# Sums of squares per row tile in column strips of TensorE, with partial adds of squares on GpSimd and VectorE, in the ternary feed-forward stages

## The chip, the core and the metric

The kernel runs on one core of a Trainium2 chip. The core has a matrix engine (PE, TensorE), three engines for elementwise work (DVE, VectorE; ACT, ScalarE; POOL, GpSimd) and a queue engine for transfers (SP, SyncE). The engines run their own instruction lists in order and meet at semaphores. The metric is the device time of one execution in microseconds.

## The reference

A residual stream `x` of 4096 rows (2 x 2048) by 256 passes through four stages: two layers of retention with a feed-forward part, a ternary feed-forward stage, windowed attention, and the ternary feed-forward stage again. The change is in the two ternary stages:

```
def _ternary_linear(x, w):
    alpha = jnp.mean(jnp.abs(w))
    w_t = jnp.sign(w) * (jnp.abs(w) > 0.5 * alpha).astype(w.dtype)
    w_q = w + jax.lax.stop_gradient(w_t - w)
    d = x.shape[-1]
    rms = jnp.sqrt(jnp.sum(x * x, axis=-1, keepdims=True)) / jnp.sqrt(jnp.asarray(d, x.dtype))
    x_norm = x / (rms + EPS)
    return jnp.einsum('bsd,fd->bsf', x_norm, w_q)
h = jax.nn.gelu(_ternary_linear(x, w_up), approximate=False)
return _ternary_linear(h, w_down)
```

The second product needs, for each of the 4096 rows, the mean of the squares of its 1024 hidden values. The kernel multiplies first and divides each output row by its rms afterwards.

## The kernel before

The function `ffn` is one stage. The names in the profile that begin with `ternary_ffn` belong to its two ternary calls. The 4096 rows are worked through in 8 blocks of 512 (`BT`); a block is 4 row tiles of 128. The hidden width of 1024 is 8 pieces of 128, counted by `m`. Hidden values stand transposed: 128 hidden channels on the partitions, 512 rows of the stream along the free axis.

Each engine has its own block of code with the same loop: `g` counts steps, `b = g - 2` is the block in work, `m` runs from 0 to 7. What an engine does, and in which order, is written out by hand with conditions on `m`; semaphores join the engines.

- PE, per `m`: `up_product(b, m)` (4 matmuls of 512 columns into `hp`, L679), then `down_product(b, m - 2)` (8 matmuls of 256 columns into `yp`, L690); for `m` of 0 and 1 it is the previous block's down products 6 and 7. Between them, at chosen `m`, stand the transposes of the next block's input (`tp`, L706), the sums of squares (`sqp`, L717) and the transposes of those sums (L724).
- ACT: `hidden` reads `hp` twice (L595 to `h`, L596 to `h_hi`); `odd_square` squares the pieces of odd `m` into `h_sq`; `sums_out` moves the sums to the SBUF tile `sq_sums`.
- DVE: `hidden_low` makes `h_lo = h - h_hi` (L433), which `down_product` needs; `residual` (L462) adds the finished block to the stream at the head of the block two later; `normalise` makes `xn` (L426); `statistics` and `aggregate` (L410, L418) go before the next block's scale; `mean_square` (L445).
- POOL: `even_square` squares the pieces of even `m` (L354); `squared_scales` and `last_scale` (L319 to L347) make the next block's scale; `rows_rms` (L359, L363) makes the rms that `residual` waits for.

The sums of squares. `h_sq` is 8 pieces of 128 x 512. `square_sums` has two halves of four pieces. In each, piece `s` of the half is the moving operand of one matmul with 32 columns of ones as weights, so that it uses one strip of 32 columns of the PE array and writes partitions `32 s` to `32 s + 31` of the bank `sqp`. After both halves strip `s` holds the sums over pieces `s` and `4 + s` for all 512 rows. ACT moves the bank, four transposes turn it, and a DVE reduction adds the four strips.

Of the kernel before, what the change touches and what calls it, by code (L numbers as in the profile page):

```python
# [25 lines left out]
P = 128  # L26
# [81 lines left out]
def ffn(nc, name, X, ident, lane, *, up, down, norm=None, hidden_bias=None, out_bias=None,  # L108
# [11 lines left out]
    with ExitStack() as c:  # L120
# [16 lines left out]
        if ternary:  # L137
            table_set = sb("table_set", [P, 1])
            h_sq = sb("h_sq", [P, MF, BT])
            sq_sums = sb("sq_sums", [P, BT])  # L140
# [47 lines left out]
        act_sq = sem("act_sq")  # L188
        sq_used = sem("sq_used")
# [80 lines left out]
        def _(pool):  # L270
# [85 lines left out]

            def rows_rms(b):
# [20 lines left out]
            def body(i):  # L378
                for k in range(2):
# [10 lines left out]
                    for m in range(0, MF, 2):  # L390
                        if live(b, NB):
                            even_square(b, m)
                        if m == 2 and unmeasured(g):
# [4 lines left out]
                        if m == 4 and live(b - 1, NB):  # L398
                            rows_rms(b - 1)
# [4 lines left out]
        def _(dve):  # L404
# [36 lines left out]

            def mean_square(b):
                dve.wait_ge(ms_full, b + 1)
                at_least(dve, rms_work, 2 * b - 1)
                nc.vector.tensor_reduce(ms[:, :], sqp[:, :].rearrange("p (t s e) -> p t s e", t=TB, e=SEG)[:, :, :, 0],  # L445
                                        axis=AX.X, op=ALU.add).then_inc(ms_done, 1)
# [98 lines left out]
            def body(i):  # L545
                for k in range(2):
                    g = 2 * i + k
                    b = g - 2
                    for m in range(MF):
# [32 lines left out]
        def _(act):  # L582
# [61 lines left out]
            def body(i):  # L644
                for k in range(2):
                    g = 2 * i + k
                    b = g - 2
                    for m in range(MF):
# [8 lines left out]
                        if m == 2 and ternary and live(b - 1, NB):  # L657
# [11 lines left out]
        def _(pe):  # L669
# [70 lines left out]
            def body(i):  # L740
                for k in range(2):
                    g = 2 * i + k
                    b = g - 2
                    for m in range(MF):
                        if live(b, NB):
                            up_product(b, m, k)
                        if ternary and m == (1 if last_block(b) else 2) and live(b - 1, NB):
# [5 lines left out]
                        if ternary and m == 4 and live(b - 1, NB):  # L753
# [1613 lines left out]
```

## Time and profile before

| | us |
|---|---|
| median of 3 runs | 1574.1 |
| the runs | 1572.0, 1574.1, 1576.66 |
| the profiled execution, its own time | 1573.14 |
| its span in the trace | 1571.4 |
| PE busy in the span | 1470.7 |
| DVE, ACT, POOL busy | 1020.5, 918.7, 765.0 |
| mean granted clock of TensorE | 0.973 of full |

The span is the time from the first to the last instruction of the profiled execution. Busy time of PE contains the pipeline latency of each matmul, so starts of successive rows tell more than durations. "Idle before" stands in brackets with what ended it. Columns of the timeline: start, duration, engine, line, operation, output and inputs, count. The ternary stages lie at about 913 to 1066 us and 1414 to 1571 us.

### The profile page before, as it was taken

What the parts mean: (1) busy time and instruction counts of PE and PEld (TensorE: products, weight loads), DVE (VectorE), ACT (ScalarE), POOL (GpSimd) and SP (SyncE); (2) the same over time, 40 slices, a digit from 0 to 9 for tenths busy, and PEclk for the clock granted to TensorE, in tenths of its full rate; (3) what the DMA queues carried; (4) which work ended last, traced back from release to release, by engine and by line L of the source; (5) the groups of instructions that cost most, each with busy time, mean ns of one, the idle gap of its engine ahead of it and who ended that gap; (6) DMA issues with size and microseconds to landing.
All of it is one profiled execution on the core that took longest, in us unless ns stands there. A gap on an engine that the chain in (4) does not pass through costs nothing. (4 is left out here: it accounts for less than half of the span.)

```text
span 1571.4 us, 36208 instructions
## 1 busy us (share of the span) xinstructions
PE 1470.7 (94%) x12834; PEld 1202.5 (77%) x12834; DVE 1020.5 (65%) x2266; ACT 918.7 (58%) x1728; POOL 765.0 (49%) x826
## 2 busy tenths in 40 slices
PE   4999997999998999997999989995999999989998
PEld 3777875889886788876989878884777777768786
DVE  4877775554436877874655757663777777756664
ACT  4565553555544555445555556663777777756665
POOL 2566765111104666664313335543666666635553
PEclk9999998899999999998999999997999999999999
DMA  7000000100001000002000010000000000000101
GB/s 238 2 2 1 0 1 1 34 1 1 1 1 55 2 2 0 2 1 94 28 28 14 1 38 1 0 1 1 1 1 0 0 0 0 1 1 1 41 27 42
DMA packets 21089, 26.17 MB, mean 17 GB/s; under 512 B 1904, under 2 KB 19056, under 8 KB 20848
## 3 DMA queue, kind: packets, MB, share of 16 engines
q1 hardware_dynamic: 18432, 21.64, 4.1%
q10 hardware_dynamic: 2544, 3.04, 0.6%
q8 instruction: 69, 1.13, 0.3%
q14 instruction: 44, 0.36, 0.1%
HBM read 20.48 MB, written 4.19 MB: 16 GB/s over the span
## 5 line engine op out<-in xcount | busy, mean ns | idle before, releaser
L595 ACT ACTIVATE ffn_h<-ffn_hp,c_b 128x512 f32<-128x512 f32 x128 | 88.3, 690 | 171.5 <-PE ffn_hp L679 171.2
L433 DVE TENSOR_TENSOR ffn_h_lo<-ffn_h,ffn_h_hi 128x512 fp32r<-128x512 f32 x128 | 93.7, 732 | 144.1 <-ACT ffn_h_hi L596 144.0
L433 DVE TENSOR_TENSOR ternary_ffn_h_lo<-ternary_ffn_h,ternary_ffn_h_hi 128x512 fp32r<-128x512 f32 x128 | 97.7, 763 | 110.4 <-ACT ternary_ffn_h_hi L596 109.6
L690 PE MATMUL ffn_yp<-down_hi,ffn_h_hi 128*128 128x256 f32 x512 | 145.5, 284 | 0.0
L690 PE MATMUL ffn_yp<-down_hi,ffn_h_lo 128*128 128x256 f32 x512 | 142.8, 279 | 0.0
L690 PE MATMUL ffn_yp<-down_lo,ffn_h_hi 128*128 128x256 f32 x512 | 142.8, 279 | 0.0
L690 PE MATMUL ternary_ffn_yp<-down_ternary,ternary_ffn_h_hi 128*128 128x256 f32 x512 | 132.7, 294 | 0.0
L986 POOL TENSOR_TENSOR ret_qk<-ret_qk,ret_qk_sin 128x512 f32<-128x512 f32 x64 | 82.7, 1292 | 102.6 <-DVE ret_qk_sin L1083 101.9
L595 ACT ACTIVATE ternary_ffn_h<-ternary_ffn_hp 128x512 f32<-128x512 f32 x128 | 76.6, 598 | 95.8 <-PE ternary_ffn_hp L679 91.7
L354 POOL TENSOR_TENSOR ternary_ffn_h_sq<-ternary_ffn_h 128x512 f32<-128x512 f32 x64 | 79.4, 1241 | 105.3 <-ACT ternary_ffn_h_hi L596 105.3
L690 PE MATMUL ternary_ffn_yp<-down_ternary,ternary_ffn_h_lo 128*128 128x256 f32 x512 | 125.5, 280 | 0.0
L992 POOL TENSOR_TENSOR ret_rstd<-ret_sums,ret_minus_half 128x16 f32<-128x16 f32 x32 | 103.7, 3241 | 44.0 <-DVE ret_sums L1125 44.0
L1710 POOL TENSOR_TENSOR wa_rms<-wa_rms,win_minus_half 128x20 f32<-128x20 f32 x32 | 119.1, 3722 | 2.7
L690 PEld LDWEIGHTS ternary_ffn_yp<-down_ternary,ternary_ffn_h_hi 128*128 128x128 f32 x512 | 96.9, 189 | 29.2 <-issue 26.0
L1930 ACT ACTIVATE wa_probs_t<-wa_tp 128x512 f32<-128x512 f32 x128 | 76.4, 597 | 62.7 <-PE wa_tp L2100 62.2
L679 PE MATMUL ternary_ffn_hp<-xt_hi,up_ternary 128*128 128x512 f32 x256 | 103.7, 405 | 4.3 <-DVEq L578 4.3
L679 PE MATMUL ffn_hp<-xt_hi,up_hi 128*128 128x512 f32 x256 | 102.6, 401 | 4.4 <-DVEq L578 4.4
L679 PE MATMUL ternary_ffn_hp<-xt_lo,up_ternary 128*128 128x512 f32 x256 | 103.9, 406 | 0.0
L679 PE MATMUL ffn_hp<-xt_lo,up_hi 128*128 128x512 f32 x256 | 102.4, 400 | 0.0
L308 POOL TENSOR_SCALAR ffn_scale_work<-mean_var 128x4 f32<-128x4 f32 x13 | 3.6, 280 | 202.5 <-DVE mean_var L418 202.5
L679 PE MATMUL ffn_hp<-xt_hi,up_lo 128*128 128x512 f32 x256 | 102.0, 398 | 0.0
L690 PEld LDWEIGHTS ffn_yp<-down_lo,ffn_h_hi 128*128 128x128 f32 x512 | 96.4, 188 | 4.3
(265 smaller groups left out, 4619.6 us busy)
## 6 DMA issues: line engine op xcount, KB each, us to landing
X<-in_x SPq DMA_DIRECT2D x8, 512.0 KB, 10.1
staging<-in_w SPq DMA_DIRECT2D x4, 1024.0 KB, 9.1
ffn_x_in<-in_x SPq DMA_DIRECT2D x8, 512.0 KB, 3.8
out<-X SPq DMA_DIRECT2D x7, 512.0 KB, 2.9
rotary<-in_rotary ACTq DMA_DIRECT2D x1, 1024.0 KB, 7.2
staging<-in_w_up SPq DMA_DIRECT2D x1, 1024.0 KB, 4.8
staging<-in_w_down SPq DMA_DIRECT2D x1, 1024.0 KB, 8.2
staging<-in_wqkv ACTq DMA_DIRECT2D x1, 768.0 KB, 6.0
```

The costliest lines, as they stand in the source:

```text
L308: nc.gpsimd.tensor_scalar(work[:, 0, :], mv[:, k, :, 1], EPS, None, ALU.add).then_inc(work_done, 1)
L354: nc.gpsimd.tensor_tensor(h_sq[:, m, :], h[:, m % R, :], h[:, m % R, :], ALU.mult).then_inc(pool_sq, 1)
L433: nc.vector.tensor_tensor(h_lo[:, m % R, :], h[:, m % R, :], h_hi[:, m % R, :].bitcast(F32), ALU.subtract).then_inc(h_ready, 1)
L595: nc.scalar.activation(h[:, m % R, :], hp[m % 2][:, :], fn, bias=bias)
L679: last = nc.tensor.matmul(hp[m % 2][:, :], w[:, j, m * P:(m + 1) * P], x[:, k, j, :], start=(n == 0), stop=(n == len(todo) - 1))
L690: last = nc.tensor.matmul(yp[k][t // 2][:, (t % 2) * D:(t % 2 + 1) * D], x[:, m % R, t * P:(t + 1) * P], w[:, m, :], start=(m == 0 and t % ...
L986: nc.gpsimd.tensor_tensor(qk[:, r, :, :, :], qk[:, r, :, :, :], qk_sin[:, r, :, :, :], ALU.add).then_inc(qk_done, 1)
L992: nc.gpsimd.tensor_tensor(rstd[:, :], sums[:, 1, :], minus_half[:, :], ALU.pow).then_inc(rstd_done, 1)
L1710: nc.gpsimd.tensor_tensor(rms[:, 1, :], rms[:, 0, :], minus_half[:, :], ALU.pow).then_inc(rms_work, 1)
L1930: nc.scalar.activation(pt[:, g, :, :].rearrange("p c n -> p (c n)"), tp[:, :], ACT.Copy).then_inc(pt_done, 1)
```

## The change

- Squares are added before PE sums them. POOL adds piece 1 onto 0 (`add_01`, behind the square of piece 2) and then 2 onto 0 (`add_0123`, behind the square of piece 4) and 5 onto 4 (`add_45`). DVE adds 3 onto 2 (`add_23`, at `m` of 4), and, in the next block at `m` of 1, 7 onto 6 and 6 onto 4 (`add_67`, `add_4567`). In the last block of a stage the second half is not added: PE reads its four pieces.
- `square_sums` takes one added piece per half. Row tile `t` of it (128 columns) goes to strip `t`, in place of piece `s` (512 columns) to strip `s`. The sums stand in the first 128 columns of `sqp`.
- One transpose turns them, in place of four; ACT moves 128 x 128; DVE copies four columns (`tensor_copy`) in place of the reduction.
- Places: PE's second half moves from `m` of 2 to 3, the transpose from 4 to 5, the first half from 6 to 7; `sums_out` from 2 to 4, `mean_square` from 4 to 5, `rows_rms` from 4 to 6.

```
+            def add_01(b):
+                pool.wait_ge(pool_sq, MF // 2 * b + 1)
+                pool.wait_ge(act_sq, MF // 2 * b + 1)
+                nc.gpsimd.tensor_tensor(h_sq[:, 0, :], h_sq[:, 0, :], h_sq[:, 1, :], ALU.add).then_inc(sq_01, 1)
+
+            def add_0123(b):
+                pool.wait_ge(sq_01, b + 1)
+                pool.wait_ge(sq_23, b + 1)
+                nc.gpsimd.tensor_tensor(h_sq[:, 0, :], h_sq[:, 0, :], h_sq[:, 2, :], ALU.add).then_inc(sq_0123, 1)
+
+            def add_45(b):
+                pool.wait_ge(pool_sq, MF // 2 * b + 3)
+                pool.wait_ge(act_sq, MF // 2 * b + 3)
+                nc.gpsimd.tensor_tensor(h_sq[:, 4, :], h_sq[:, 4, :], h_sq[:, 5, :], ALU.add).then_inc(sq_45, 1)
...
                         if live(b, NB):
                             even_square(b, m)
+                            if m == 2:
+                                add_01(b)
+                            if m == 4:
+                                add_0123(b)
+                                if not final_block(b):
+                                    add_45(b)
...
-                        if m == 4 and live(b - 1, NB):
+                        if m == 6 and live(b - 1, NB):
                             rows_rms(b - 1)
...
+            def add_23(b):
+                dve.wait_ge(pool_sq, MF // 2 * b + 2)
+                dve.wait_ge(act_sq, MF // 2 * b + 2)
+                nc.vector.tensor_tensor(h_sq[:, 2, :], h_sq[:, 2, :], h_sq[:, 3, :], ALU.add).then_inc(sq_23, 1)
+
+            def add_67(b):
+                dve.wait_ge(pool_sq, MF // 2 * (b + 1))
+                dve.wait_ge(act_sq, MF // 2 * (b + 1))
+                nc.vector.tensor_tensor(h_sq[:, 6, :], h_sq[:, 6, :], h_sq[:, 7, :], ALU.add).then_inc(sq_67, 1)
+
+            def add_4567(b):
+                dve.wait_ge(sq_45, b + 1)
+                dve.wait_ge(sq_67, b + 1)
+                nc.vector.tensor_tensor(h_sq[:, 4, :], h_sq[:, 4, :], h_sq[:, 6, :], ALU.add).then_inc(sq_4567, 1)
...
-                nc.vector.tensor_reduce(ms[:, :], sqp[:, :].rearrange("p (t s e) -> p t s e", t=TB, e=SEG)[:, :, :, 0],
-                                        axis=AX.X, op=ALU.add).then_inc(ms_done, 1)
+                nc.vector.tensor_copy(ms[:, :], sqp[:, 0:P].rearrange("p (t e) -> p t e", e=SEG)[:, :, 0]
+                                      ).then_inc(ms_done, 1)
...
-                        if m == 4 and ternary and live(b - 1, NB):
+                        if m == 5 and ternary and live(b - 1, NB):
                             mean_square(b - 1)
+                        if m == 4 and ternary and live(b, NB):
+                            add_23(b)
+                        if m == 1 and ternary and live(b - 1, NB) and not final_block(b - 1):
+                            add_67(b - 1)
+                            add_4567(b - 1)
...
             def square_sums(b, half):
 
-                done = MF // 2 * b + 2 * (half + 1)
-                pe.wait_ge(act_sq, done)
-                pe.wait_ge(pool_sq, done)
+                if half == 1 and final_block(b):
+                    pe.wait_ge(act_sq, MF // 2 * (b + 1))
+                    pe.wait_ge(pool_sq, MF // 2 * (b + 1))
+                    whole_rows = (4, 5, 6, 7)
+                else:
+                    pe.wait_ge(sq_4567 if half else sq_0123, b + 1)
+                    whole_rows = (4 * half,)
                 if half == 0:
                     at_least(pe, ms_done, b)
-                for s in range(4):
-                    last = nc.tensor.matmul(sqp[SEG * s:SEG * (s + 1), :], ones[:, :], h_sq[:, 4 * half + s, :],
-                                            start=(half == 0), stop=(half == 1))
+                for m in whole_rows:
+                    for t in range(TB):
+                        last = nc.tensor.matmul(sqp[SEG * t:SEG * (t + 1), 0:P], ones[:, :], h_sq[:, m, t * P:(t + 1) * P],
+                                                start=(half == 0), stop=(half == 1 and m == whole_rows[-1]))
                 last.then_inc(sums_full if half else sq_used, 1)
...
-                        if ternary and m == (1 if last_block(b) else 2) and live(b - 1, NB):
+                        if ternary and m == (1 if last_block(b) else 3) and live(b - 1, NB):
                             square_sums(b - 1, 1)
```

DVE at the head of a block of the first ternary stage, from the reciprocal for `residual` to the second pair of `statistics`, before:

```order
L451 RECIPROCAL ternary_ffn_inv_rms<-ternary_ffn_rms 128x4
L462 SCALAR_TENSOR_TENSOR X<-ternary_ffn_yp,ternary_ffn_inv_rms,X 128x256 x4
L433 TENSOR_TENSOR ternary_ffn_h_lo<-ternary_ffn_h,ternary_ffn_h_hi 128x512
L426 TENSOR_SCALAR xn<-X,mean_var,scale 128x256 x4
L433 TENSOR_TENSOR ternary_ffn_h_lo<-ternary_ffn_h,ternary_ffn_h_hi 128x512
L410 BN_STATS ternary_ffn_stats<-X 128x6 x2
L433 TENSOR_TENSOR ternary_ffn_h_lo<-ternary_ffn_h,ternary_ffn_h_hi 128x512
L410 BN_STATS ternary_ffn_stats<-X 128x6 x2
L418 BN_AGGR mean_var<-ternary_ffn_stats 128x2 x4
```

and now:

```order
L494 RECIPROCAL ternary_ffn_inv_rms<-ternary_ffn_rms 128x4
L505 SCALAR_TENSOR_TENSOR X<-ternary_ffn_yp,ternary_ffn_inv_rms,X 128x256 x4
L461 TENSOR_TENSOR ternary_ffn_h_lo<-ternary_ffn_h,ternary_ffn_h_hi 128x512
L454 TENSOR_SCALAR xn<-X,mean_var,scale 128x256 x4
L461 TENSOR_TENSOR ternary_ffn_h_lo<-ternary_ffn_h,ternary_ffn_h_hi 128x512
L438 BN_STATS ternary_ffn_stats<-X 128x6 x2
L478 TENSOR_TENSOR ternary_ffn_h_sq<-ternary_ffn_h_sq 128x512
L483 TENSOR_TENSOR ternary_ffn_h_sq<-ternary_ffn_h_sq 128x512
L461 TENSOR_TENSOR ternary_ffn_h_lo<-ternary_ffn_h,ternary_ffn_h_hi 128x512
L438 BN_STATS ternary_ffn_stats<-X 128x6 x2
L446 BN_AGGR mean_var<-ternary_ffn_stats 128x2 x4
L461 TENSOR_TENSOR ternary_ffn_h_lo<-ternary_ffn_h,ternary_ffn_h_hi 128x512
```

The adds L478 (`add_67`) and L483 (`add_4567`) now stand between the first pair of `statistics` and `h_lo` of piece 2.

POOL from the squares of pieces 0 and 2 on (`x2`), before; the row ahead of them is `last_scale`:

```order
L347 TENSOR_TENSOR scale<-ternary_ffn_scale_work,ternary_ffn_powers 128x4
L354 TENSOR_TENSOR ternary_ffn_h_sq<-ternary_ffn_h 128x512 x2
L319 TENSOR_SCALAR ternary_ffn_scale_work<-mean_var 128x4
L320 TENSOR_TENSOR ternary_ffn_scale_work<-mean_var,ternary_ffn_powers 128x4
L322 TENSOR_TENSOR ternary_ffn_scale_work<-ternary_ffn_scale_work,ternary_ffn_powers 128x4
L326 TENSOR_SCALAR ternary_ffn_scale_work<-ternary_ffn_scale_work 128x4
L329 TENSOR_TENSOR ternary_ffn_scale_work<-ternary_ffn_scale_work 128x4
L354 TENSOR_TENSOR ternary_ffn_h_sq<-ternary_ffn_h 128x512
L359 TENSOR_TENSOR ternary_ffn_rms<-ternary_ffn_mean_square,ternary_ffn_powers 128x4
L363 TENSOR_SCALAR ternary_ffn_rms<-ternary_ffn_rms 128x4
```

and now, without the row of `last_scale`:

```order
L361 TENSOR_TENSOR ternary_ffn_h_sq<-ternary_ffn_h 128x512 x2
L367 TENSOR_TENSOR ternary_ffn_h_sq<-ternary_ffn_h_sq 128x512
L326 TENSOR_SCALAR ternary_ffn_scale_work<-mean_var 128x4
L327 TENSOR_TENSOR ternary_ffn_scale_work<-mean_var,ternary_ffn_powers 128x4
L329 TENSOR_TENSOR ternary_ffn_scale_work<-ternary_ffn_scale_work,ternary_ffn_powers 128x4
L333 TENSOR_SCALAR ternary_ffn_scale_work<-ternary_ffn_scale_work 128x4
L336 TENSOR_TENSOR ternary_ffn_scale_work<-ternary_ffn_scale_work 128x4
L361 TENSOR_TENSOR ternary_ffn_h_sq<-ternary_ffn_h 128x512
L372 TENSOR_TENSOR ternary_ffn_h_sq<-ternary_ffn_h_sq 128x512
L377 TENSOR_TENSOR ternary_ffn_h_sq<-ternary_ffn_h_sq 128x512
L361 TENSOR_TENSOR ternary_ffn_h_sq<-ternary_ffn_h 128x512
L381 TENSOR_TENSOR ternary_ffn_rms<-ternary_ffn_mean_square,ternary_ffn_powers 128x4
```

Three adds over the tile of squares are new (L367, L372, L377), and the rms L381 stands behind the square of piece 6, not of piece 4.

PE around the second half of the sums, before (behind up product 2):

```order
L679 MATMUL ternary_ffn_hp<-xt_hi,up_ternary 128x512
L679 MATMUL ternary_ffn_hp<-xt_lo,up_ternary 128x512
L712 ISA
L717 MATMUL ternary_ffn_sqp<-ternary_ffn_h_sq,ternary_ffn_ones 32x512 x4
L690 MATMUL ternary_ffn_yp<-down_ternary,ternary_ffn_h_hi 128x256
L690 MATMUL ternary_ffn_yp<-down_ternary,ternary_ffn_h_lo 128x256
```

and now (behind up product 3; `tp` are the transposes of the next block's input):

```order
L727 MATMUL ternary_ffn_hp<-xt_hi,up_ternary 128x512
L727 MATMUL ternary_ffn_hp<-xt_lo,up_ternary 128x512
L770 MATMUL ternary_ffn_sqp<-ternary_ffn_h_sq,ternary_ffn_ones 32x128 x4
L754 MATMUL ternary_ffn_tp<-c_ident,xn 128x128 x4
L738 MATMUL ternary_ffn_yp<-down_ternary,ternary_ffn_h_hi 128x256
L738 MATMUL ternary_ffn_yp<-down_ternary,ternary_ffn_h_lo 128x256
```

The group now stands one up product and one down product later, ahead of the input's transposes, and its matmuls have 128 columns.

## Rows read from the trace of the kernel before

**Rows 1.** The page: busy time and granted clock in 40 slices

```profile
PE 1470.7 (94%) x12834; PEld 1202.5 (77%) x12834; DVE 1020.5 (65%) x2266; ACT 918.7 (58%) x1728; POOL 765.0 (49%) x826
...
PEclk9999998899999999998999999997999999999999
```

**Rows 2.** The table by stretches: one block of the first ternary stage

```profile
core 0: us, PE busy (x) PEld busy (x) DVE busy (x) ACT busy (x) POOL busy (x), PEclk, DMA share, GB/s
990.67:1009.30 18.63, 18.63 (x127) 14.81 (x125) 12.18 (x28) 12.48 (x24) 9.91 (x13) 1.00 0.00 0
```

**Rows 3.** Timeline of PE (start, duration; idle before in brackets)

```profile
990.67 0.40 PE L679 MATMUL ternary_ffn_hp<-xt_hi,up_ternary 128*128 128x512 f32 x1
...
992.52 0.40 PE L679 MATMUL ternary_ffn_hp<-xt_hi,up_ternary 128*128 128x512 f32 x1
...
995.08 0.40 PE L679 MATMUL ternary_ffn_hp<-xt_lo,up_ternary 128*128 128x512 f32 x1
995.41 1.06 PE L717 MATMUL ternary_ffn_sqp<-ternary_ffn_h_sq,ternary_ffn_ones 128*32 128x512 f32 x8
996.41 0.39 PE L690 MATMUL ternary_ffn_yp<-down_ternary,ternary_ffn_h_hi 128*128 128x256 f32 x1
996.63 0.28 PE L690 MATMUL ternary_ffn_yp<-down_ternary,ternary_ffn_h_lo 128*128 128x256 f32 x1
996.75 0.28 PE L690 MATMUL ternary_ffn_yp<-down_ternary,ternary_ffn_h_hi 128*128 128x256 f32 x1
```

**Rows 4.** Timeline of PE, a cut of 0.1 us at the start of one group

```profile
986.77 0.64 PE L717 MATMUL ternary_ffn_sqp<-ternary_ffn_h_sq,ternary_ffn_ones 128*32 128x512 f32 x4
```

**Rows 5.** Timeline of PE, the four transposes of the sums

```profile
1000.69 0.60 PE L724 MATMUL ternary_ffn_sqp<-c_ident,ternary_ffn_sq_sums 128*128 128x128 f32 x4
1001.04 0.36 PE L690 MATMUL ternary_ffn_yp<-down_ternary,ternary_ffn_h_hi 128*128 128x256 f32 x1
```

**Rows 6.** Timeline of DVE over the head of that block

```profile
992.17 1.66 DVE L462 SCALAR_TENSOR_TENSOR X<-ternary_ffn_yp,ternary_ffn_inv_rms,X 128x256 f32 x4 [0.25 <-DVE ternary_ffn_inv_rms L451]
993.75 1.05 DVE L433 TENSOR_TENSOR ternary_ffn_h_lo<-ternary_ffn_h,ternary_ffn_h_hi 128x512 fp32r<-128x512 f32 x1
994.73 1.37 DVE L426 TENSOR_SCALAR xn<-X,mean_var,scale 128x256 f32 x4
...
996.63 0.73 DVE L410 BATCH_NORM_STATS2 ternary_ffn_stats<-X 128x6 f32 x2
997.29 1.19 DVE L433 TENSOR_TENSOR ternary_ffn_h_lo<-ternary_ffn_h,ternary_ffn_h_hi 128x512 fp32r<-128x512 f32 x1
```

**Rows 7.** Timeline of POOL over the same block

```profile
993.22 1.04 POOL L354 TENSOR_TENSOR ternary_ffn_h_sq<-ternary_ffn_h 128x512 f32<-128x512 f32 x1 [2.48 <-ACT ternary_ffn_h_hi L596]
996.89 1.04 POOL L354 TENSOR_TENSOR ternary_ffn_h_sq<-ternary_ffn_h 128x512 f32<-128x512 f32 x1 [2.63 <-ACT ternary_ffn_h_hi L596]
999.95 0.61 POOL L319 TENSOR_SCALAR ternary_ffn_scale_work<-mean_var 128x4 f32<-128x4 f32 x1 [2.02 <-DVE mean_var L418]
...
1004.32 1.04 POOL L359 TENSOR_TENSOR ternary_ffn_rms<-ternary_ffn_mean_square,ternary_ffn_powers 128x4 f32<-128x4 f32 x1
```

**Rows 8.** Timelines of DVE and of POOL where both start together

```profile
988.15 0.69 DVE L433 TENSOR_TENSOR ternary_ffn_h_lo<-ternary_ffn_h,ternary_ffn_h_hi 128x512 fp32r<-128x512 f32 x1 [1.08 <-ACT ternary_ffn_h_hi L596]
...
988.20 1.54 POOL L354 TENSOR_TENSOR ternary_ffn_h_sq<-ternary_ffn_h 128x512 f32<-128x512 f32 x1 [1.09 <-ACT ternary_ffn_h_hi L596]
```

**Rows 9.** Groups by form on POOL: busy, mean ns of one, idle before

```profile
L986 POOL TENSOR_TENSOR ret_qk<-ret_qk,ret_qk_sin 128x512 f32<-128x512 f32 x64 | 82.7, 1292 | 102.6 <-DVE ret_qk_sin L1083 101.9
L354 POOL TENSOR_TENSOR ternary_ffn_h_sq<-ternary_ffn_h 128x512 f32<-128x512 f32 x64 | 79.4, 1241 | 105.3 <-ACT ternary_ffn_h_hi L596 105.3
```

**Rows 10.** Stretches at 910 us, and PE's timeline there

```profile
910.00:913.40 3.40, 1.28 (x9) 1.04 (x9) 1.32 (x2) 0.77 (x1) 0.79 (x6) 0.99 0.00 0
913.40:916.80 3.40, 3.40 (x10) 2.61 (x9) 0.69 (x1) 2.19 (x5) 2.58 (x5) 0.50 0.88 266
...
912.93 0.50 PE L679 MATMUL ternary_ffn_hp<-xt_hi,up_ternary 128*128 128x512 f32 x1 [2.12 <-DVEq L578]
```

More of the change, by code:

```diff
@@ L95, in last_block, with final_block @@
     return isinstance(b, int) and b == NB
+def final_block(b):
+    return isinstance(b, int) and b == NB - 1
 def after_last(b):
@@ L139, in ffn @@
             h_sq = sb("h_sq", [P, MF, BT])
-            sq_sums = sb("sq_sums", [P, BT])
+            sq_sums = sb("sq_sums", [P, P])
             ones = sb("ones", [P, SEG])
@@ L188, in ffn @@
         act_sq = sem("act_sq")
+        sq_01, sq_23, sq_0123 = sem("sq_01"), sem("sq_23"), sem("sq_0123")
+        sq_45, sq_67, sq_4567 = sem("sq_45"), sem("sq_67"), sem("sq_4567")
         sq_used = sem("sq_used")
@@ L623, in sums_out @@
                 at_least(act, ms_full, b)
-                nc.scalar.activation(sq_sums[:, :], sqp[:, :], ACT.Copy, scale=1.0 / FF).then_inc(sums_moved, 1)
+                nc.scalar.activation(sq_sums[:, :], sqp[:, 0:P], ACT.Copy, scale=1.0 / FF).then_inc(sums_moved, 1)
             def for_next_stage(g, m):
@@ L656, in body @@
                             odd_square(b, m)
-                        if m == 2 and ternary and live(b - 1, NB):
+                        if m == 4 and ternary and live(b - 1, NB):
                             sums_out(b - 1)
@@ L722, in transpose_sums @@
                 pe.wait_ge(sums_moved, b + 1)
-                for t in range(TB):
-                    last = nc.tensor.transpose(sqp[:, t * P:(t + 1) * P], sq_sums[:, t * P:(t + 1) * P], ident[:, :])
-                last.then_inc(ms_full, 1)
+                nc.tensor.transpose(sqp[:, 0:P], sq_sums[:, :], ident[:, :]).then_inc(ms_full, 1)
             def weight_total():
@@ L752, in body @@
                             transposes(g - 1, 1)
-                        if ternary and m == 4 and live(b - 1, NB):
+                        if ternary and m == 5 and live(b - 1, NB):
                             transpose_sums(b - 1)
-                        if ternary and m == 6 and live(b, NB):
+                        if ternary and m == 7 and live(b, NB):
                             square_sums(b, 0)
```

## The prediction

> **What bounds the kernel now.** I read the page first: PE is busy 1470.7 of 1571.4 us and is granted close to full clock nearly everywhere [rows 1]. The table by stretches then shows one block of a ternary stage, from the start of one up product 0 to the next: 18.63 us, PE busy in all of them at a clock of 1.00, DVE 12.2, ACT 12.5, POOL 9.9 [rows 2]. So PE's own work sets a block, and an instruction taken from PE is time won for as long as nothing else makes PE wait. An up product and the down product behind it take 992.52 - 990.67 = 1.85 us, 0.93 and 0.92 [rows 3]. Eight pairs make 14.8 us; the other 3.8 are the two groups of sums, two groups of input transposes and the group of four transposes of the sums.
>
> **What PE saves.** A group of sums: the last matmul of the up product starts at 995.08 and the group at 995.41; 0.23 would be the usual step (0.93 / 4), so 0.10 is lost there. The next down matmul starts at 996.41 and its second 0.22 later where 0.12 is usual [rows 3]. The group costs 0.10 + 1.00 + 0.10 = 1.20 us. Four matmuls start within 0.64 - 0.60 = 0.04 us of each other [rows 4] (0.60 is one such matmul's duration), so the strips run side by side, and the eight records are two passes. Of the 1.00, two passes of 512 columns would take 2 x 0.43 = 0.86 if a column is worth what one lasts at 1.00 less the tail of 0.14. With 128 columns a pass is a quarter: 0.21. A group then costs 1.20 - 0.64 = 0.56. The bounds: the saving is at most 0.86 (the columns free), and it is at least 0.30 if eight short matmuls can start no faster than those four transposes do, 0.35 / 4 = 0.09 each [rows 5], 0.70 in all in place of 1.00. I take 0.64, since four starts within 0.04 us are the nearest row. Three of four transposes go: 3 x 0.09 = 0.26 [rows 5]. A block so loses 2 x 0.64 + 0.26 = 1.54 us of PE work: 17.1 in place of 18.63. Over 16 blocks that would be 24 us, were nothing late.
>
> The Trainium skill, page "TensorE: Matmul & The Clock Gate", section "Wait — 56ns, not 53.3ns?", says that with hardware decoding off the sequencer spends about 62 ns on each matmul and that this binds once the array's work is shorter. By it eight records would take 0.50 and the saving would be 0.36 a group, some 9 us less over both stages; the row with four starts in 0.04 us speaks against it, though those may have been decoded ahead.
>
> **What is late: the second half of the sums.** Count from the start of up product 0 (t = 0, 990.67 in the rows). PE now asks for `sq_4567` after four up and three down products, t = 4 x 0.93 + 3 x 0.92 = 6.5. DVE has to do `add_67` and `add_4567` before that, behind the first pair of `statistics`. In the rows that pair is done, and the next instruction starts, at 997.29, t = 6.6 [rows 6]. So even with nothing in the way the two adds end at t = 8.0: each is 0.69 as `h_lo` alone [rows 8], the first 0.61 up to the next start (`xn` starts 0.07 ahead of the end of `h_lo` [rows 6]), and I allow 0.1 for the hand-overs by semaphore. So PE waits 1.5 us. That alone eats the 1.54.
>
> And something is in the way. DVE's `h_lo` and POOL's square, both with 128x512 operands in SBUF, don't run at once: POOL's square lasts 1.04 alone [rows 7], and 1.54 where DVE began 0.05 before it [rows 8]; DVE's `h_lo` lasts 0.69 alone [rows 8], and 1.05 and 1.19 where POOL's squares of 993.22 and 996.89 were under way [rows 6, 7]: each ends about 0.6 behind the end of the square. The adds on either engine are of this form. POOL's square of piece 2 holds from t = 6.2 to 7.2 [rows 7], and `add_01` is queued right behind it with all its inputs ready. So from t = 7.2 `add_67`, `add_01` and `add_4567` go one after another, in whichever order. For `add_01` I have two rows: 1.04 for a square, whose two inputs are one tile, and 1.29 for `ret_qk`, a sum of two tiles of this size [rows 9]; it is the second that an add resembles: 1.29. The sum: 7.2 + 0.61 + 1.29 + 0.69 + 0.1 = 9.9. PE waits 3.4 us, between 1.5 (nothing shared) and 4.1 (all of DVE 0.7 later, as `residual` is below).
>
> The Trainium skill, page "SBUF — State Buffer", section "Who interferes with whom", states this as an exclusive lock on a port pair for a DVE instruction with two SBUF inputs against a GpSimd one that reads SBUF. The rows above agree. By a kernel in which they shared bandwidth, the wait would be nearer to 1.5.
>
> **What is queued behind.** `h_lo` of piece 2 waits on DVE behind the adds, to about t = 10.6 in place of 7.8, the statistics and the aggregate behind it too, and with them POOL's scale, which began at 999.95, t = 9.3 [rows 7], and now begins near 12. POOL then has squares 4 and 6, two adds of 1.29 and the rms, about 6 us, back to back, with 3.4 us of scale ahead: the rms moves from 13.7 (1004.32) [rows 7] to the first microseconds of the next block. `residual`, which starts at t = 1.5 now (992.17) [rows 6], starts near 2.2, and `h_lo` of piece 0 behind it is some 0.3 us late for its down product. ACT's narrower move, DVE's copy and the later places of both are hidden under PE's products: they cost nothing as long as the rms is there by the head of the next block, else the sum above.
>
> **The sum.** A full block: 18.63 - 1.54 + 3.4 + 0.3 = 20.8, 2.15 more than before. Each stage has six such blocks (the second halves of blocks 1 to 6): 12 x 2.15 = 26. Block 0's half comes where DVE has no `residual` yet, so its wait is nearer 1.5: nothing gained or lost. The final block asks for no adds in its second half and saves one group and the transposes, 0.9, twice: -2. Together +24 us.
>
> **The clock.** After PE had stood for 2.12 us before 912.93, the granted clock was 0.50, that is 1.2 GHz, for the next 3.4 us [rows 10]. A wait of 3.4 each block shows as an idle of some 3.2, longer than that one. If each of the 12 costs a stretch of 3.4 us at half clock, up to 1.7 us of work is lost each time, less what of the stretch lies in the wait itself. I take 0.9: +11 us. The bounds are 0 and 20.
>
> Profiled execution 1573.1 + 24 + 11 = 1608; the median stands 1 us above it, so 1609.
>
> **Rivals.**
> (a) As forecast, 1600 to 1620: chance 0.45.
> (b) The same waits, but shorter or without the fall of the clock: `add_01` at 1.04 and a wait of 3.1 gives 1573 + 12 x 1.8 - 2 = 1593; waits as forecast and full clock give 1598. 1579 to 1600: chance 0.33.
> (c) Faster. DVE reaches the adds earlier, or the adds of the two engines don't hold each other up. If PE's wait is 0.8 where I have 3.4, a block is 17.9, and 14 blocks x -0.7 - 2 = -13: 1561. It turns at a wait of 1.5 us. What speaks for it: PE's new order gives all engines other phases, and in the rows DVE has idle time of its own (12.2 busy of 18.63). Against it: that idle time is not at the head of a block, where `residual`, `xn` and `statistics` fill it from 992.17 to 997.29 [rows 6]. 1550 to 1569: chance 0.17.
> (d) The wait is about 1.5 and nothing changes, 1570 to 1579: 0.05.
>
> About 0.3%, 5 us, is what a measurement of this kernel can tell from no change. Slower by more than that: 0.45 + 0.33 = 0.78; within it 0.05; faster 0.17. The range of 1573 to 1620 leaves out (c) and the ends of (a) and (d), about 0.2.
>
> **What the profile after would show.** Right: a group of sums at 0.2 to 0.35 us between its start and the next; PE's stop before `sqp` in the second half, released by a DVE add over `h_sq`, some 3 us, 12 times, and about 1.5 twice; blocks of 20.5 to 22.5 us; DVE's adds stretched beyond 0.69 beside POOL's of about 1.3; stretches of clock 0.50 behind the stops. Wrong if: blocks are 17 to 18 us; POOL's adds last 1.04; the clock stays at 1.00 through the stops; or PE stops elsewhere, at `h_lo` for instance.

## The result, and the profile after

The changed kernel takes 1605.1 us (median of 4 runs, 1600.3 to 1606.5), the kernel before 1573.05 beside it: a ratio of 1.0198, 95% interval 1.0165 to 1.0231. It is slower by 32 us, and the interval lies clear of 1; forecast was 1609, with 0.78 on slower. Its profiled execution took 1603.9, the span is 1602.0 us.

The page, the lines of [rows 1]:

```profile
PE 1458.0 (91%) x12802; PEld 1208.4 (75%) x12834; DVE 1085.5 (68%) x2310; ACT 914.9 (57%) x1728; POOL 838.7 (52%) x872
...
PEclk9999997999999999979999989997999999999998
```

PE is busy 12.7 us less and yet the span is 30.6 longer; DVE gained 65 us of work, POOL 74. The table by stretches, from one second group of sums to the next, which is one block as in [rows 2] (twice in the first ternary stage, once in the second):

```profile
core 0: us, PE busy (x) PEld busy (x) DVE busy (x) ACT busy (x) POOL busy (x), PEclk, DMA share, GB/s
966.89:988.91 22.02, 18.86 (x121) 15.87 (x121) 16.09 (x32) 12.15 (x23) 15.67 (x15) 0.92 0.01 1
988.91:1010.63 21.72, 17.27 (x121) 14.38 (x121) 16.91 (x32) 12.26 (x23) 14.61 (x15) 1.00 0.00 1
1477.61:1498.22 20.61, 17.26 (x121) 14.37 (x121) 16.08 (x32) 12.26 (x23) 15.72 (x15) 1.00 0.08 27
```

A block took 18.63; now 20.6 to 22.0, of which PE works 17.3 at full clock. Where it stands, from PE's timeline (start, duration, idle before in brackets), beside [rows 3] and [rows 4]:

```profile
966.89 0.43 PE L770 MATMUL ternary_ffn_sqp<-ternary_ffn_h_sq,ternary_ffn_ones 128*32 128x128 f32 x8 [2.86 <-DVE ternary_ffn_h_sq L483]
...
978.79 0.39 PE L727 MATMUL ternary_ffn_hp<-xt_hi,up_ternary 128*128 128x512 f32 x1
...
983.99 0.39 PE L738 MATMUL ternary_ffn_yp<-down_ternary,ternary_ffn_h_hi 128*128 128x256 f32 x1 [0.38 <-DVE ternary_ffn_h_lo L461]
...
988.91 0.42 PE L770 MATMUL ternary_ffn_sqp<-ternary_ffn_h_sq,ternary_ffn_ones 128*32 128x128 f32 x8 [2.78 <-DVE ternary_ffn_h_sq L483]
989.27 0.44 PE L754 MATMUL ternary_ffn_tp<-c_ident,xn 128*128 128x128 f32 x2
...
1005.04 0.38 PE L738 MATMUL ternary_ffn_yp<-down_ternary,ternary_ffn_h_hi 128*128 128x256 f32 x1 [0.99 <-DVE ternary_ffn_h_lo L461]
...
1010.63 0.42 PE L770 MATMUL ternary_ffn_sqp<-ternary_ffn_h_sq,ternary_ffn_ones 128*32 128x128 f32 x8 [3.46 <-DVE ternary_ffn_h_sq L483]
```

The group itself is short (0.36 to the next start, 1.00 before). Ahead of it PE stands until `add_4567` (L483) is done, and at the head of the block it also stands at down product 0, for `h_lo`. The view of the tile `h_sq` counts the first kind and gives each add's least, median and longest duration:

```profile
L367 POOL TENSOR_TENSOR ternary_ffn_h_sq<-ternary_ffn_h_sq x16: 1307/1707/1741, 922.0 to 1582.7; 128x512 f32<-128x512 f32 x16
...
L377 POOL TENSOR_TENSOR ternary_ffn_h_sq<-ternary_ffn_h_sq x14: 1284/1293/1741, 932.9 to 1572.7; 128x512 f32<-128x512 f32 x14
L478 DVE TENSOR_TENSOR ternary_ffn_h_sq<-ternary_ffn_h_sq x14: 667/864/1444, 941.4 to 1580.4; 128x512 f32<-128x512 f32 x14
L483 DVE TENSOR_TENSOR ternary_ffn_h_sq<-ternary_ffn_h_sq x14: 691/1566/1568, 942.7 to 1581.2; 128x512 f32<-128x512 f32 x14
...
  PE ternary_ffn_sqp L770: 37.1, 13
```

DVE's timeline at the end of the stretch before 988.91, beside [rows 6]:

```profile
981.60 1.66 DVE L505 SCALAR_TENSOR_TENSOR X<-ternary_ffn_yp,ternary_ffn_inv_rms,X 128x256 f32 x4 [0.25 <-DVE ternary_ffn_inv_rms L494]
...
985.66 0.74 DVE L438 BATCH_NORM_STATS2 ternary_ffn_stats<-X 128x6 f32 x2
986.33 0.87 DVE L478 TENSOR_TENSOR ternary_ffn_h_sq<-ternary_ffn_h_sq 128x512 f32<-128x512 f32 x1
987.30 1.56 DVE L483 TENSOR_TENSOR ternary_ffn_h_sq<-ternary_ffn_h_sq 128x512 f32<-128x512 f32 x1
```

and POOL's, beside [rows 7]:

```profile
980.90 0.23 POOL L385 TENSOR_SCALAR ternary_ffn_rms<-ternary_ffn_rms 128x4 f32<-128x4 f32 x1 [0.22 <-POOL ternary_ffn_rms L381]
...
985.03 1.61 POOL L361 TENSOR_TENSOR ternary_ffn_h_sq<-ternary_ffn_h 128x512 f32<-128x512 f32 x1 [1.88 <-ACT ternary_ffn_h_hi L644]
986.61 1.70 POOL L367 TENSOR_TENSOR ternary_ffn_h_sq<-ternary_ffn_h_sq 128x512 f32<-128x512 f32 x1
```

`add_67` ends at 987.20, 0.56 behind the end of POOL's square (986.64); `add_4567` ends at 988.86, 0.55 behind the end of `add_01` (988.31), and PE starts 0.05 later. Of PE's three microseconds DVE needs 1.4 for the adds alone (two of 0.69); the rest is DVE and POOL taking turns. DVE's `statistics`, just ahead of them, kept their 0.74 although POOL's square ran beside them.

### The profile page after: what moved, and what is told of

Same layout as the page of the kernel before. It is cut to its first block and busy times, and to the rows that moved or that the text cites. A ratio compares the mean times of both kernels' runs of the same rounds, so it can differ in the third digit from the quotient of the medians.

```text
span 1602.0 us, 36348 instructions
## 1 busy us (share of the span) xinstructions
PE 1458.0 (91%) x12802; PEld 1208.4 (75%) x12834; DVE 1085.5 (68%) x2310; ACT 914.9 (57%) x1728; POOL 838.7 (52%) x872
## 5 line engine op out<-in xcount | busy, mean ns | idle before, releaser
L461 DVE TENSOR_TENSOR ternary_ffn_h_lo<-ternary_ffn_h,ternary_ffn_h_hi 128x512 fp32r<-128x512 f32 x128 | 110.8, 869 | 61.5 <-ACT ternary_ffn_h_hi L644 61.5
L738 PE MATMUL ternary_ffn_yp<-down_ternary,ternary_ffn_h_hi 128*128 128x256 f32 x512 | 136.9, 300 | 4.0 <-DVE ternary_ffn_h_lo L461 4.0
L738 PE MATMUL ternary_ffn_yp<-down_ternary,ternary_ffn_h_lo 128*128 128x256 f32 x512 | 130.2, 288 | 0.0
L738 PEld LDWEIGHTS ternary_ffn_yp<-down_ternary,ternary_ffn_h_hi 128*128 128x128 f32 x512 | 101.8, 199 | 15.3 <-DVE X L505 5.2
L361 POOL TENSOR_TENSOR ternary_ffn_h_sq<-ternary_ffn_h 128x512 f32<-128x512 f32 x64 | 84.3, 1317 | 49.0 <-ACT ternary_ffn_h_hi L644 48.9
L738 PEld LDWEIGHTS ternary_ffn_yp<-down_ternary,ternary_ffn_h_lo 128*128 128x128 f32 x512 | 101.7, 199 | 3.2
## 6 DMA issues: line engine op xcount, KB each, us to landing
X<-in_x SPq DMA_DIRECT2D x8, 512.0 KB, 10.1
```

The costliest lines, as they stand in the source:

```text
L361: nc.gpsimd.tensor_tensor(h_sq[:, m, :], h[:, m % R, :], h[:, m % R, :], ALU.mult).then_inc(pool_sq, 1)
L461: nc.vector.tensor_tensor(h_lo[:, m % R, :], h[:, m % R, :], h_hi[:, m % R, :].bitcast(F32), ALU.subtract).then_inc(h_ready, 1)
L738: last = nc.tensor.matmul(yp[k][t // 2][:, (t % 2) * D:(t % 2 + 1) * D], x[:, m % R, t * P:(t + 1) * P], w[:, m, :], start=(m == 0 and t % ...
```

## The experiments

In all of them the places of the groups, the transpose, `sums_out`, `mean_square` and `rows_rms` are those of the change unless the diff says otherwise; times are medians; each ratio is against the kernel before, timed beside that run, with its 95% interval.

**No adds.** PE reads all four pieces of each half, in column strips, with one transpose.

```
-                            if m == 2:
-                                add_01(b)
...
-                if half == 1 and final_block(b):
-                    pe.wait_ge(act_sq, MF // 2 * (b + 1))
-                    pe.wait_ge(pool_sq, MF // 2 * (b + 1))
-                    whole_rows = (4, 5, 6, 7)
+                if True:
+                    pe.wait_ge(act_sq, MF // 2 * b + 2 * (half + 1))
+                    pe.wait_ge(pool_sq, MF // 2 * b + 2 * (half + 1))
+                    whole_rows = tuple(range(4 * half, 4 * half + 4))
```

> Row tiles in strips, one transpose, and every place moved as in the change, but no adds: PE reads four pieces in each half (16 matmuls of 128 columns). Theory A (the adds make PE wait): PE's groups cost as before, 1.2 us, three transposes a block go, 16 x 0.26 = 4 us, so 1569 and no wait of PE on the sums. Rival C (the later places of the rms, the move and the transpose delay `residual` and with it everything): waits of PE on `h_lo` or on xn stay and the time is 1580 or more. Rival B (more and narrower matmuls are dearer than counted, sequencer-bound): the group takes 2 us or more in place of 1.0, the time 1590 or more.

1565.34 against 1572.19: 0.9961 (0.9949 to 0.9974). A block in the table by stretches:

```profile
988.20:1006.41 18.21, 18.21 (x177) 15.73 (x173) 12.80 (x28) 12.26 (x24) 10.30 (x13) 1.00 0.00 0
```

The second half's group in PE's timeline:

```profile
996.61 1.08 PE L759 MATMUL ternary_ffn_sqp<-ternary_ffn_h_sq,ternary_ffn_ones 128*32 128x128 f32 x32
997.62 0.55 PE L743 MATMUL ternary_ffn_tp<-c_ident,xn 128*128 128x128 f32 x3
```

A group lasts 1.01, as before: 32 records in place of 8, with a quarter of the columns each. The block loses 0.42, where the three transposes explain 0.26; the other 0.16 comes with the places. The late places of the sums and of the rms alone cost nothing: PE shows no wait for the sums or for `h_lo` in this run's ternary stages.

**Adds in the first half only** (`add_01`, `add_23`, `add_0123`; the second half whole).

```
-                                if not final_block(b):
-                                    add_45(b)
...
-                            add_67(b - 1)
-                            add_4567(b - 1)
...
+                if half == 1:
```

> The change, with the adds of the first half alone (two on POOL, one on DVE); the second half is read whole by PE, 16 matmuls of 128 columns. Theory A: nothing is added at the head of a block, where DVE is full, so PE waits for no add; a block loses 0.64 + 0.26 = 0.9 us, 16 blocks 14 us: 1559, at full clock through the ternary stages. Rival A' (it is the port pair taken by any add, wherever it stands, that costs): DVE's h_lo and POOL's squares of pieces 4 to 6 get late, and the time stays at 1575 or above. Rival C: as in the run without adds, 1580 or more.

1562.82, 0.9942 (0.9925 to 0.9959). Blocks are a steady 17.57, so narrowing a group is worth 18.21 - 17.57 = 0.64. One block, the second of the first ternary stage, took 22.9: PE stood for `add_0123` there. In PE's timeline:

```profile
956.15 0.43 PE L765 MATMUL ternary_ffn_sqp<-ternary_ffn_h_sq,ternary_ffn_ones 128*32 128x128 f32 x8 [3.08 <-POOL ternary_ffn_h_sq L372]
```

and in POOL's, 7 us earlier:

```profile
949.04 3.14 POOL L329 TENSOR_TENSOR ternary_ffn_scale_work<-ternary_ffn_scale_work,ternary_ffn_powers 128x4 f32<-128x4 f32 x1
```

L329 normally lasts 1.01. In that block DVE also mixes the next stage's weights (L552), so that from 948.39 to 951.65 it ran instructions with two inputs without a pause.

**Adds in the second half only** (`add_45`, `add_67`, `add_4567`; the first half whole).

```
+                if half == 0 or final_block(b):
```

> The change, with the adds of the second half alone (one on POOL behind the square of piece 4, two on DVE at m of 1); the first half is read whole. Theory A: the wait before the second half's sums stays, about 2 to 2.5 us (no add_01 between the two DVE adds any more, and POOL is free earlier), 12 times, with some falls of the clock: 1573 - 14 + 12 x 2.2 + 5 = 1590. Rival A' (the number of adds counts, not where): half of the change's loss, less than 1582.

1589.54, 1.0117 (1.01 to 1.0134). This half alone loses 17 us, about half of the change's 32, where the first half alone gained 9. PE waits 2.0 in most blocks (13 waits, 1.1 to 2.0, together 23.8), although `add_01` is gone. With the first half's adds put back the 13 waits are 37.1: adds that gain when they stand alone cost 16 us (1589.5 to 1605.1) beside the second half's. So the second half alone makes half of the loss, and the other half arises only where both are present. Two neighbouring blocks in the table by stretches, alike but for the clock:

```profile
963.91:983.54 19.63, 17.62 (x145) 15.06 (x145) 14.10 (x31) 12.14 (x23) 11.57 (x13) 1.00 0.01 3
983.54:1004.71 21.17, 19.18 (x145) 16.59 (x146) 13.96 (x31) 12.25 (x23) 12.11 (x13) 0.92 0.00 0
```

A fall of the clock behind the wait costs 21.17 - 19.63 = 1.54 us.

**The six adds over 4 of their 512 columns**: the instructions, waits and places stay, the work goes. What is summed is no longer the squares of all pieces: only 4 of 512 rows get all of them, in this run and the next two each for the adds that are cut.

```
-                nc.gpsimd.tensor_tensor(h_sq[:, 0, :], h_sq[:, 0, :], h_sq[:, 1, :], ALU.add).then_inc(sq_01, 1)
+                nc.gpsimd.tensor_tensor(h_sq[:, 0, 0:4], h_sq[:, 0, 0:4], h_sq[:, 1, 0:4], ALU.add).then_inc(sq_01, 1)
```

> The change with its order, semaphores and narrow groups, but each of the six adds works on 4 of 512 columns, so the sums leave out most of the squares' adds. Theory A: the adds' work is what PE waits for; with 0.1 us each PE waits 0.2 us a block at most, and the narrow groups show their worth: 1573 - 24 + 4 = 1553. Rival D (the new waits and hand-overs by semaphore cost, not the work): 1575 or more. Rival B: the narrow group saves less than 0.64, then 1560 or more with no wait of PE.

1557.21, 0.9903 (0.9887 to 0.992). PE still waits; a block in the table by stretches:

```profile
980.41:998.34 17.93, 16.99 (x122) 14.45 (x122) 12.23 (x32) 12.17 (x24) 10.66 (x15) 1.00 0.00 1
```

Its end in PE's timeline:

```profile
998.34 0.43 PE L770 MATMUL ternary_ffn_sqp<-ternary_ffn_h_sq,ternary_ffn_ones 128*32 128x128 f32 x8 [0.94 <-DVE ternary_ffn_h_sq L483]
```

and in DVE's:

```profile
997.55 0.47 DVE L478 TENSOR_TENSOR ternary_ffn_h_sq<-ternary_ffn_h_sq 128x4 f32<-128x4 f32 x1
998.12 0.16 DVE L483 TENSOR_TENSOR ternary_ffn_h_sq<-ternary_ffn_h_sq 128x4 f32<-128x4 f32 x1
```

and in POOL's:

```profile
996.96 1.04 POOL L361 TENSOR_TENSOR ternary_ffn_h_sq<-ternary_ffn_h 128x512 f32<-128x512 f32 x1 [2.44 <-ACT ternary_ffn_h_hi L644]
```

PE falls idle at 998.34 - 0.94 = 997.40 and DVE reaches the adds 0.15 later. The first one lasts 0.47, though such a short add lasts 0.15 where nothing holds it: it ends just behind POOL's square (998.00). That hold, the late start and the hand-overs are the 0.9 above the 16.99 of work. There are 12 such waits, together 10.3 us where I had allowed 4, which more than covers the 4 us that I missed (the saving was larger too). The full adds cost 1605.1 - 1557.2 = 48 us; waits and hand-overs by semaphore alone don't make the loss.

**Only POOL's adds over 4 columns, and only DVE's.** The same edit, to three adds each.

> The change with POOL's three adds over 4 of 512 columns (so the sums leave those adds out) and DVE's three adds whole. With all six short the block was 17.9 us, with PE waiting about 1.1 for DVE's adds. Theory A (both DVE's own queue and POOL's add between): DVE's two adds bring 2 x 0.6 more, so PE waits about 2.3 and a block is 19.1; some waits are followed by a fall of the clock: 1578, between 1572 and 1585. Rival (POOL's adds are nothing, it is DVE's alone): as the change, 1600 or more. Rival (only the clash matters): as all short, 1557 to 1562.

> The change with DVE's three adds over 4 of 512 columns and POOL's three whole. Theory A: DVE's short adds still queue behind POOL's square of piece 2 and add_01 (up to 1.04 + 1.29) and `xn` and the rms stay late, so PE waits 1.5 to 2.5 a block: 1575, between 1566 and 1585. Rival (it is DVE's time that counts): 1557 to 1562. Rival (it is POOL's time alone): 1595 or more.

1584.66, 1.0081 (1.0064 to 1.0098), and 1582.38, 1.0068 (1.0051 to 1.0085). DVE's adds alone cost 27 us over those with all six cut, POOL's alone 25; together 48. Neither queue is the whole cause. With DVE's adds alone, in PE's timeline:

```profile
982.16 0.43 PE L770 MATMUL ternary_ffn_sqp<-ternary_ffn_h_sq,ternary_ffn_ones 128*32 128x128 f32 x8 [2.01 <-DVE ternary_ffn_h_sq L483]
```

and in DVE's:

```profile
980.08 1.23 DVE L478 TENSOR_TENSOR ternary_ffn_h_sq<-ternary_ffn_h_sq 128x512 f32<-128x512 f32 x1
981.41 0.69 DVE L483 TENSOR_TENSOR ternary_ffn_h_sq<-ternary_ffn_h_sq 128x512 f32<-128x512 f32 x1
```

With POOL's adds alone, in PE's timeline:

```profile
1004.10 0.48 PE L770 MATMUL ternary_ffn_sqp<-ternary_ffn_h_sq,ternary_ffn_ones 128*32 128x128 f32 x8 [2.49 <-DVE ternary_ffn_h_sq L483]
```

in DVE's:

```profile
999.28 2.10 DVE L454 TENSOR_SCALAR xn<-X,mean_var,scale 128x256 f32 x4
1001.30 1.76 DVE L461 TENSOR_TENSOR ternary_ffn_h_lo<-ternary_ffn_h,ternary_ffn_h_hi 128x512 fp32r<-128x512 f32 x1
```

and in POOL's:

```profile
1000.19 1.04 POOL L361 TENSOR_TENSOR ternary_ffn_h_sq<-ternary_ffn_h 128x512 f32<-128x512 f32 x1 [1.38 <-ACT ternary_ffn_h_hi L644]
1001.19 1.32 POOL L367 TENSOR_TENSOR ternary_ffn_h_sq<-ternary_ffn_h_sq 128x512 f32<-128x512 f32 x1
```

`h_lo` takes 1.76 and ends 0.55 behind POOL's `add_01`, and what queues behind it is late. The medians lie 6.7 and 7.4 above what I expected. The waits were about as long as I had taken them (2.0 in most blocks with DVE's adds, 1.7 to 1.9 and once 2.5 with POOL's); in the profiled executions 6 and 8 of them were followed by a stretch at the clock's lower level, which I had priced low. How much of the 7 us is the clock's isn't separated, and the profiled execution with DVE's adds alone, 1579.65, is itself 5 below its median.

**DVE's second-half adds ahead of the first pair of `statistics`.** This asks whether what stands ahead of the adds in DVE's queue (Theory A) makes the wait.

```
+                        if m == 1 and ternary and live(b - 1, NB) and not final_block(b - 1):
+                            add_67(b - 1)
+                            add_4567(b - 1)
                         if 1 <= m < 3 and unmeasured(g):
                             statistics(g, 2 * m - 2)
```

> The change with add_67 and add_4567 ahead of the first pair of statistics on DVE instead of behind. Theory A (PE waits for what stands ahead of the adds on DVE): the two statistics of 0.67 us together come off the wait, 12 times, and a fall of the clock or two may go: 1605 - 8 - 3 = 1594. Rival (the moment is set by POOL's square of piece 2 and add_01 on the port pair): nothing gained, 1602 to 1608.

1602.87, 1.0195 (1.0178 to 1.0212): 2 us less than the change where Theory A gave 11. DVE's timeline in one block:

```profile
1005.36 2.17 DVE L454 TENSOR_SCALAR xn<-X,mean_var,scale 128x256 f32 x4
1007.45 1.75 DVE L461 TENSOR_TENSOR ternary_ffn_h_lo<-ternary_ffn_h,ternary_ffn_h_hi 128x512 fp32r<-128x512 f32 x1
1009.13 0.68 DVE L478 TENSOR_TENSOR ternary_ffn_h_sq<-ternary_ffn_h_sq 128x512 f32<-128x512 f32 x1
```

The 0.7 us of `statistics` are no longer ahead, but `h_lo` now meets POOL's square and `add_01` (`h_lo` 1.75 for 0.69), so the adds begin no sooner. That holds for this block and four like it, where PE waited 2.8 to 3.0 as before. In the others the new place did help; two waits in PE's timeline:

```profile
956.13 0.44 PE L770 MATMUL ternary_ffn_sqp<-ternary_ffn_h_sq,ternary_ffn_ones 128*32 128x128 f32 x4 [3.08 <-POOL ternary_ffn_h_sq L372]
...
1032.47 0.32 PE L770 MATMUL ternary_ffn_sqp<-ternary_ffn_h_sq,ternary_ffn_ones 128*32 128x128 f32 x4 [1.73 <-DVE ternary_ffn_h_sq L483]
```

The waits for `add_4567` fell from 37.1 to 25.5 us in all (12 of them, seven between 1.0 and 1.9). About half of that came back elsewhere: 3.1 for `add_0123` in block 1 (the wait before 956.13), 1.8 more for `h_lo` and 0.9 more for the first `xn`; where the rest went isn't traced. So the place in DVE's queue sets part of the wait, which the median alone would hide.

**The first half added, but for block 1**, where the weights are mixed: `first half only` with that block whole.

```
+                            if m == 2 and not second_block(b):
+                                add_01(b)
...
+                if half == 1 or second_block(b):
```

> The version with the first half's adds alone, in which PE waited 3.1 us once: block 1 of the first ternary stage, where DVE also mixes the attention weights and POOL's power took 3.1 us. Here block 1 of each stage is read whole in both halves. If that one wait and the clock's fall behind it are what held that version back: 1562.8 - 3.1 - 1.5 + 2 x 0.64 = 1559.5. If not: 1562 or above.

1557.68 (1556.27 to 1558.0), 0.9901 (0.9885 to 0.9918): faster than both kernels, by 15 us and 47. Against the run without adds (1565.34) the first half's adds are worth 8 or 9 of the 15; the rest is the one transpose and the places. In the table by stretches a block has PE at work throughout:

```profile
978.80:996.37 17.57, 17.57 (x153) 15.09 (x149) 13.07 (x30) 12.17 (x24) 13.43 (x15) 1.00 0.00 0
```

**That, with `add_45` on POOL too**; PE reads three pieces in the second half. (In block 1's second half piece 5 is left out of the sum.)

```
+                    if half == 1 and not final_block(b) and not second_block(b):
+                        pe.wait_ge(sq_45, b + 1)
+                        whole_rows = (4, 6, 7)
```

> The version with the first half's adds (block 1 whole), and POOL's add_45 besides, so that PE reads three pieces (4 with 5 added, 6, 7) in the second half of all blocks but 1 and the last. Each saves PE 0.21 us, 12 times 2.6 us, so 1555 if nothing is late. Rival: POOL has 1.3 to 1.7 us more ahead of the square of piece 6, the rms and the scale; the rms, for which DVE already waits 0.6 at the head of a block, moves 1.3 later, `residual` and the first h_lo with it, and PE waits for h_lo: 1558 or above. I hold this rival likelier, since POOL's add stands where the rms is next.

1573.1 against 1573.25, 0.9998 (0.9989 to 1.0006). One more add on POOL (1.27 at the least, 1.74 in the median of its 12) eats the whole gain of 15 us, without any of DVE's second-half adds. Nothing waits for `add_45` itself: down product 0 stands for `h_lo` (9 waits, 9.6 us in all), and the first half's group of the same block for `add_0123` (L377, 2.9 us in all), which comes later on POOL than before. In PE's timeline:

```profile
996.75 0.38 PE L746 MATMUL ternary_ffn_yp<-down_ternary,ternary_ffn_h_hi 128*128 128x256 f32 x1 [1.26 <-DVE ternary_ffn_h_lo L470]
...
1009.01 0.43 PE L781 MATMUL ternary_ffn_sqp<-ternary_ffn_h_sq,ternary_ffn_ones 128*32 128x128 f32 x8 [0.40 <-POOL ternary_ffn_h_sq L377]
```

**The change with the rms ahead of `add_45`** and of the square of piece 6.

```
                                 add_0123(b)
-                                if not final_block(b):
-                                    add_45(b)
+                        if m == 4 and live(b - 1, NB):
+                            rows_rms(b - 1)
+                        if m == 4 and live(b, NB) and not final_block(b):
+                            add_45(b)
```

> The change with the rms on POOL ahead of add_45 and of the square of piece 6, in place of behind both. In the change DVE waited 1.67 us at the head of a block for the rms. Theory A (the late rms is part of what makes DVE's adds late): the residual starts up to 1.5 us sooner, PE's wait before the second half's sums falls by about as much where DVE's own order allows, 12 blocks x 0.7: about 1594. Rival A'' (the port pair and POOL's square of piece 2 set the moment of DVE's adds, whenever the residual starts): 1602 or above. A side effect: add_45 is later, and if add_4567 comes to wait for it, PE's wait grows.

1596.16, 1.014 (1.0126 to 1.0155): with the rms early 9 us of the loss go. A block in the table by stretches:

```profile
968.10:988.12 20.02, 17.22 (x121) 14.37 (x121) 15.98 (x32) 12.14 (x23) 14.68 (x15) 1.00 0.01 2
```

A wait in PE's timeline, two blocks on:

```profile
1008.13 0.65 PE L770 MATMUL ternary_ffn_sqp<-ternary_ffn_h_sq,ternary_ffn_ones 128*32 128x128 f32 x8 [2.81 <-DVE ternary_ffn_h_sq L483]
```

The waits for `h_lo` are gone but for one of 0.44, which is 3.5 us less; the 13 waits for the adds are 36.1 in all, 37.1 in the change (2.8 in most blocks, 3.3 to 3.6 in three). The profiled execution, 1602.18, is the slowest of the four and 6 above the median, so the trace can't show the rest of the 9. The wait for the adds doesn't hang on the rms, since `residual` (999.94) is early and DVE then meets POOL's square and `add_01` all the same (`add_67` 0.86, `add_4567` 1.57).

## Why the prediction was right

The mechanism and nearly every term held; the forecast was 4 us high. Some of that closeness is luck: set against the forecast, the saving was 2.5 us larger, the waits for the adds 4.5 shorter (with 1.5 for each block 0), those for `h_lo` 1.9 longer, a wait for the first `xn`, which I had not counted, 1.4 longer, and the clock about as priced, so the misses partly cancel.

- **PE's saving, forecast 1.54 a block.** Measured 1.70: a group 0.64 as forecast (first half only), the transposes and places 0.42 where I had 0.26 (no adds). Over 14 blocks, and 1.06 in each final block: -25.9.
- **The wait for the adds, forecast 3.4, twelve times.** 13 waits show 37.1; the twelve long ones 2.94 each, and with the part that the last matmul's latency hides (0.40 - 0.23 = 0.17) 3.1. Together 37.1 + 13 x 0.17 = +39.3. In the block from 978.79 PE fell idle at t = 7.3 and the adds were done at t = 10.1, where I had 6.5 and 9.9. On PE's side I had left out that its stop at `h_lo` comes first; on the other side POOL's square ended at t = 7.9 in place of 7.2, while the three adds behind it took 2.2 in place of 2.6, as `add_67` had begun beside the square. The count was right and its place not: block 0 has the full wait in both stages (2.86 at 944.28, 2.66 at 1456.01) although no `residual` stands ahead, and block 6, the last one with adds, has 1.83 and none. `residual` is thus not needed for the full wait.
- **The shared path.** Shown from both sides: DVE's adds without POOL's leave a wait of 2.0 in most blocks, POOL's without DVE's one of 1.7 to 1.9 (2.5 once), both together 2.9, none 0.9. `add_01` lasts at least 1.31 in the changed kernel, nearer to `ret_qk` [rows 9] than to the square. The Trainium skill, page "SBUF — State Buffer", section "Who interferes with whom", calls it an exclusive lock; the trace agrees for DVE's instructions with two 128x512 inputs: in the rows shown each blocked one ends 0.55 behind the end of POOL's that blocks it, however early it began (1.56 and 0.87 for the adds, 1.76 for `h_lo`), which fits waiting in turn better than both running slower.
- **`h_lo` of piece 0, forecast 0.3 each time.** Nine waits, 0.16 to 0.99, 4.0 in all (with the hidden 0.17 each, 5.5), where I had 3.6. `residual` starts at t = 2.8 (981.60 - 978.79) in place of 2.2.
- **The clock, forecast +11.** The span grew by 30.6. Taking -25.9 + 39.3 + 5.5 from it leaves 11.7; 1.4 of this is a longer wait for the first `xn` of the first ternary stage (4.49 for 3.11), so some 10 is left for the clock; it is a remainder and not measured by itself. By another way: behind 7 of the 13 waits the granted clock fell to its lower level, twice for 6.8 us and otherwise for 3.4, nine stretches; at the 1.54 of the second-half run that would be 14 at most, less what lies in a wait. PE had stood 2.86 before 966.89 and the clock fell; it had stood 2.78 before 988.91 and it did not, as the table by stretches shows:

```profile
967.30:970.70 3.40, 3.40 (x18) 3.21 (x16) 2.36 (x9) 1.12 (x2) 1.72 (x3) 0.52 0.00 0
989.30:992.70 3.40, 3.40 (x29) 3.21 (x26) 2.38 (x9) 1.84 (x4) 1.69 (x3) 1.00 0.00 0
```

My 0.9 for each of twelve was thus right as a mean of 1.5 in some and 0 in others. Which waits bring a fall stays open: no run changed the clock apart from the waits.

- **The rule on the sequencer.** I had weighed a start of a matmul each 62 ns (the Trainium skill, page "TensorE: Matmul & The Clock Gate", section "Wait — 56ns, not 53.3ns?") and chosen the trace. That was right here: 32 records start within 1.01 us in the run without adds, 0.03 each, and a narrowed group saved 0.64, not 0.36.

What the forecast did not see is that the change holds its own cure. Its first half (but for block 1), with the single transpose, is worth 15 us, as DVE and POOL have room in the middle of the block. The second half put on top takes back 47, three times that, at the head of the block, where `residual`, `xn`, `h_lo` and POOL's squares already stand in a row; alone it costs 17.

## What to carry to other kernels

When work is moved from the engine that bounds to others with idle time, ask at which moment the result is due and what stands in the queue at that moment, not what share of the time the engine idles: DVE and POOL idled a third and half of the time, and still the adds were late by 3 us in twelve of sixteen blocks. Where DVE's instructions with two inputs from SBUF, or `xn`, meet POOL's squares and adds, count their times one after the other; `statistics` beside a square kept their time. A single further add on POOL in twelve blocks took back a gain of 15 us. And where a change has two like halves, time each alone and both: the better kernel was one half of it, and the two halves cost more together than the sum of what they did alone.

## What the hardware did that I had not expected

- `xn`, with one tile from SBUF as its input, was held by POOL's instructions too. Alone its four take 1.37 [rows 6]; beside POOL's square of 1005.46 and `add_01` of 1006.46, which ended at 1007.78, they took 3.09 and ended at 1007.93. The wait of 3.46 before 1010.63 comes with this, not with slow adds (0.67 and 0.69 there). DVE's timeline:

```profile
1004.84 3.09 DVE L454 TENSOR_SCALAR xn<-X,mean_var,scale 128x256 f32 x4
...
1009.12 0.67 DVE L478 TENSOR_TENSOR ternary_ffn_h_sq<-ternary_ffn_h_sq 128x512 f32<-128x512 f32 x1
1009.89 0.69 DVE L483 TENSOR_TENSOR ternary_ffn_h_sq<-ternary_ffn_h_sq 128x512 f32<-128x512 f32 x1
```

- A POOL instruction over 4 columns was held for as long as DVE went on without a pause: 3.14 for 1.01 in the run with the first half only, the one case of this length. Small work on POOL is not safe from the shared path.
- Waits of nearly the same length (2.78, 2.86) can end with or without a fall of the clock, and waits of 2.0 brought some too, at 1.54 us each.
